# Turning a graph hop's product back: fp32 matmuls with a combining matrix, or transposes with the halves added on VectorE

## The reference, cut to what matters

```python
h0 = x @ W + b
h = h0
for _ in range(10):
    msg = (h * norm_src)[src]
    agg = segment_sum(msg, dst, num_segments=3125)
    h = 0.9 * (agg * norm_dst) + 0.1 * h0
```

## Time and profile before

| what | us |
|---|---|
| median of three runs | 3213.01 |
| lowest and highest run | 3197.84, 3217.87 |
| span of the profiled execution (first to last instruction) | 3198.0 |
| TensorE busy over the span | 2723.7 (85%) |
| VectorE busy | 2250.6 (70%) |
| ScalarE busy | 1612.0 (50%) |
| GpSimd busy | 1512.6 (47%) |

### The profile page before, as it was taken

The page is one execution under the profiler, slowest core; times in us unless marked ns, Lnnn a source line. Parts: engine busy times, 40 slices in busy tenths (PEclk is TensorE's granted clock), DMA queues, the critical chain, the costliest instruction groups (busy, mean ns, idle before and its releaser), DMA issues. The chain is left out here.

```text
span 3198.0 us, 70441 instructions
## 1 busy us (share of the span) xinstructions
PE 2723.7 (85%) x18621; PEld 1834.2 (57%) x18621; DVE 2250.6 (70%) x6702; ACT 1612.0 (50%) x4685; POOL 1512.6 (47%) x1604
## 2 busy tenths in 40 slices
PE   2777777799998499759888888998986999999998
PEld 1566665355554244337777777776874555555556
DVE  6999998566665312657777777777887777777772
ACT  1788887033332000035555555555664666666666
POOL 2121122044443000067777777777405777777770
PEclk6999999899999799869999999999997999999995
DMA  1122222056557755543333333333203555445540
GB/s 38 73 91 89 91 89 89 21 195 204 196 197 257 270 238 238 223 102 80 84 81 81 82 85 79 83 83 82 63 21 98 127 131 131 127 128 130 131 112 12
DMA packets 446966, 378.15 MB, mean 118 GB/s; under 512 B 174376, under 2 KB 385416, under 8 KB 446632
## 3 DMA queue, kind: packets, MB, share of 16 engines
q1 hardware_dynamic: 396184, 315.64, 32.3%
q0 software_dynamic: 40896, 43.60, 6.7%
q10 hardware_dynamic: 9552, 14.75, 1.3%
HBM read 286.75 MB, written 87.03 MB: 117 GB/s over the span
## 5 line engine op out<-in xcount | busy, mean ns | idle before, releaser
L1594 POOL DMA_INDIRECT big<-row_table,src x710 | 675.0, 951 | 217.1 <-issue 171.6
L2080 POOL DMA_INDIRECT big<-message_table,src x542 | 532.6, 983 | 228.2 <-issue 154.2
L2119 PE MATMUL banks<-big 128*128 128x512 f16 x1650 | 422.6, 380 | 8.9 <-DVE big L2194 8.9
L2212 DVE TENSOR_SCALAR big<-big 128x2048 f16<-128x2048 f16 (+2 forms) x396 | 422.4, 1067 | 1.3 <-DMA big<-shifted_keys 0.7
L507 PE MATMUL banks<-work 128*128 128x226 f16 x1197 | 312.3, 261 | 104.2 <-ACT banks L538 41.4
L899 PE MATMUL banks<-big,work 128*128 128x512 f16 (+1 forms) x1750 | 350.0, 359 | 17.0 <-DVE work L1041 17.0
L964 POOL TENSOR_TENSOR work<-work 128x400 f16<-128x400 f32 x196 | 180.2, 945 | 280.5 <-DVE work L1033 220.3
L1739 DVE TENSOR_REDUCE big<-banks 128x1 f32<-128x256 f32 x451 | 190.2, 422 | 173.1 <-PE banks L1637 159.7
L1637 PE MATMUL banks<-big 97*128 x902 | 303.4, 419 | 0.7
L508 PE MATMUL banks<-work 128*128 128x200 f16 x1197 | 300.5, 251 | 0.0
L509 PE MATMUL banks<-work 128*128 128x200 f16 x1197 | 298.6, 249 | 0.0
(11 more groups left out here) (373 smaller groups left out, 6143.4 us busy)
## 6 DMA issues: line engine op xcount, KB each, us to landing
big<-weights_halves SPq DMA_DIRECT2D x10, 6400.0 KB, 24.0
big<-shifted_keys SPq DMA_DIRECT2D x66, 640.0 KB
weights_dense<-work SPq DMA_DIRECT2D x196, 200.0 KB, 1.9
work<-weights_dense SPq DMA_DIRECT2D x196, 200.0 KB, 2.7
weights_halves<-work SPq DMA_DIRECT2D x98, 400.0 KB, 2.9
big<-q_table SPq DMA_DIRECT2D x451, 64.0 KB
big<-in_ef SPq DMA_DIRECT2D x403, 64.0 KB
big<-in_ea SPq DMA_DIRECT2D x403, 32.0 KB
```

The costliest lines, as they stand in the source:

```text
L1594: po.indirect_dma_start(rows[:, t % RT, s, 0:D], None, x_t.rearrange("a p c -> (a p) c"), bass.IndirectOffsetOnAxis(ap=m.src2[:, s, t:t + ...
L2080: po.indirect_dma_start(G[n % R][:, s, :], None, g_t.rearrange("a p c -> (a p) c"), bass.IndirectOffsetOnAxis(ap=m.src2[:, s, t:t + 1], ax ...
L2119: pe.matmul(psH[q % 2], table[:, a, :, :].rearrange("p s d -> p (s d)"), hot[:, 2 * TE * a:2 * TE * (a + 1)], start=(a == 0), stop=(a == N ...
L2212: dve.tensor_scalar(hot[:, 2 * TE * a:2 * TE * (a + n)], key[q % 2][:, 0:n, :], place[:, BATCHES.index((a, n)):BATCHES.index((a, n)) + 1], ...
```

## The change

The turn-back is done by transposes of 128x128 with the identity (four in a chunk of 512), so that the high halves of 128 nodes stand in 64 columns of the bank and the low halves in the next 64: a bank is now filled with 512 columns and not with 256. ScalarE multiplies in its copy by a per-partition factor `weigh`, 1 in partitions 0 to 63 and 1 / LO in the others. VectorE adds the two halves from PSUM by a tensor_reduce over a strided view (innermost the two halves, 64 columns apart) ahead of the mix. `comb` is no longer made.

```diff
+        self.weigh = self.colsN[:, 7, 10:11]
...
-            dve.tensor_copy(comb[0:D, :], m.ident[0:D, 0:D])
-            chain(dve.tensor_scalar(comb[D:P, :], m.ident[D:P, D:P], 1.0 / LO, None, ALU.mult))
+            dve.memset(m.weigh[0:D, :], 1.0)
+            dve.memset(m.weigh[D:P, :], 1.0 / LO)
...
-                    ins = pe.matmul(m.PB[6 + c % 2][0:k, i * D:(i + 1) * D], rt[c % 2][:, i * P:i * P + k], comb,
-                                    start=True, stop=True)
+                    ins = pe.transpose(m.PB[6 + c % 2][0:k, i * P:(i + 1) * P], rt[c % 2][:, i * P:i * P + k], m.ident[:, :])
...
-                    nc.scalar.copy(rt[c % 2][:, 0:width(c)], m.PB[c % 4][:, 0:width(c)]).then_inc(copied, 1)
+                    nc.scalar.activation(rt[c % 2][:, 0:width(c)], m.PB[c % 4][:, 0:width(c)], ACT.Copy, scale=m.weigh).then_inc(copied, 1)
...
-                    ps = m.PB[6 + c % 2][0:rows, 0:g * D].rearrange("p (a d) -> p a d", a=g)
+                    ps = m.PB[6 + c % 2][0:rows, 0:g * P].rearrange("p (a s d) -> p a d s", a=g, s=2)
                     tc = tmp[0:rows, 0:g, :]
...
+                    chain(dve.tensor_reduce(tc, ps, op=ALU.add, axis=X))
                     if last:
-                        chain(dve.tensor_tensor(tc, ps, sp_(c1n), ALU.mult))
+                        chain(dve.tensor_tensor(tc, tc, sp_(c1n), ALU.mult))
...
-                        chain(dve.tensor_tensor(tc, ps, sp_(c1s), ALU.mult))
+                        chain(dve.tensor_tensor(tc, tc, sp_(c1s), ALU.mult))
...
-            per = 4 * NDC
+            per = 5 * NDC
```

More of the change, by code:

```diff
@@ L682, in stage_layer0_start @@
         ones16 = small(2).bitcast(F16)
-        comb = small(3)
         buf = [m.work2[0:D, i * DC:(i + 1) * DC] for i in range(2)]
@@ L842, in stage_layer0_hops @@
         z = [m.zbuf(0), m.zbuf(1)]
-        comb = m.small(3)
         h0, hs0 = m.node(1), m.node(2)
```

## The result

| | before | with the change |
|---|---|---|
| median, us (13 runs each) | 3213.01 | 3225.41 |
| lowest and highest run | 3197.31, 3226.26 | 3210.22, 3251.76 |
| span of the profiled execution | 3198.0 | 3222.9 |
| the ten hops in it | 434.90 | 448.24 |

What follows compares the result with a forecast made beforehand. The prediction took TensorE and a nearly equally long loop through the other engines as the bound. Loop growth of 17.6 us plus 17 us of clock falls, +35 in all on the median 3213.01, gave 3248 us, range 3220 to 3280.

Steps and rivals of the forecast that it cites:

- The bound: In the ten hops: TensorE and the loop nearly equally long, so lengthening the loop is paid.
- the loop: In a hop: turn-back, mix, low halves, store, load, landing, high halves, copy, later turn-back; +0.50 us per turn-back and mix.
- TensorE's term: Turn-back on TensorE: four transposes, 0.44 us, for fp32 matmuls, 0.83 us; -0.40 us per full chunk.
- The copy's term: ScalarE's copy from PSUM, made an activation with per-partition scale: +0.085 us per copy.
- The reduce's term: VectorE's added tensor_reduce per chunk ahead of the mix: 0.86 us, +0.90 with the gap (ends 0.73 and 1.10).
- The walk over the hops: Loop growth: odd hops +1.57 us, even +0.59, degree matmul of four even hops +1.37; together +17.6 us.
- The clock's term: Longer TensorE gaps lower the granted clock: one new fall in each of seven hops, 2.4 us each, +17 us.
- The signs: Trace marks of being right, such as odd hops of 42.5 us or more and granted clock under 0.97.
- rival B: In the hops the loop grows but the clock holds: 3213 + 18 = 3231 us; chance 0.21.
- Rival A: TensorE's saving of 25 us in the hops arrives in full: 3188 us; chance 0.07.
- C: Rival: reduce of 1.06 us or more and two clock falls in each hop: +65 us, 3278 us; chance 0.15.
- D: Rival: transposes not shorter on TensorE, each loop passage losing 0.40 us more: 3253 us; chance 0.07.

Runs made afterwards that it cites:

- e6: The kernel before with ScalarE taking the high halves of chunk c behind the copy of c + 1: 3196.6 us, ratio 0.9944.
- e8: The kernel before with copies ahead of high halves, bank 4 for the small turn-back and the degree matmul a chunk later: 3189.0 us, ratio 0.9919.
- e3: The kernel before with only ScalarE's copy made a scaled activation and 1/LO taken out of the combining matrix: 3219.8 us, ratio 1.0027.
- e2: The kernel before with a useless tensor_reduce of 512 SBUF elements ahead of each mix (128 in the last chunk): 3251.9 us, ratio 1.0128.
- e5: The changed kernel with ScalarE taking the high halves of chunk c behind the copy of c + 1: 3221.9 us, ratio 1.0030.
- e4: The changed kernel with the small turn-back in its own bank 4 and the degree matmul one product later: 3213.6 us, ratio 0.9993.
- e10: e5 with seven needless matmuls ahead of turn-back 4 and eight ahead of the small one, except in the last hop: 3217.5 us, ratio 1.0011.
- e1: The changed kernel without the tensor_reduce, low halves left out of the result: 3198.4 us, ratio 0.9955.
- e7: The changed kernel with copies ahead of high halves, bank 4 for the small turn-back and the degree matmul a chunk later: 3195.6 us, ratio 0.9964.
- e9: e7 without GpSimd's wait for the mix ahead of its low halves: 3254.0 us, ratio 1.0126.

## Why the prediction was right, and where it failed

**The bound.** Right. TensorE's busy time fell by 26 us and the kernel got slower, and e6 shows the loop by undoing one link of it. "TensorE and this loop are nearly equally long now" holds too: it took e8, with ScalarE's order turned and the hop's end freed, to bring TensorE to 97%.

**TensorE's term** (-0.40 per chunk). Right: 0.44 us for 0.83.

**The copy's term** (0.085). Measured 0.10 (682 ns for 581), in the change and in e3.

**The reduce's term** (0.86, step 0.90). Mis-sized: 0.691, so a step of 0.73, my low end. I had the rows of a strided SBUF read and put PSUM half way to them; a contiguous SBUF read (e2) and the strided PSUM read cost the same to 5 ns. My walk over the loop gives +12.3 with that number and 0.10 for the copy, and the stage grew by 13.3. (The middle of my two rates, 0.69 and 1.06, is 0.87 and not 0.86; that changes nothing.) The note on cachelines that I weighed, of the Trainium skill (SBUF — State Buffer, section on the DMA port swizzle), I had read as putting the reduce at my upper end. Of PSUM the note speaks for matmuls only, and the measurement decides against my reading for this pattern.

**The walk over the hops.** The sum came out, its parts did not, so the nearness of 12.3 and 13.3 is in part luck. In two hops the clock held in both kernels, and +1.96 was forecast for either: hop 4 grew by 2.77 (41.29 to 44.06) and hop 8 by 1.40 (42.28 to 43.68). Odd hops were forecast at +1.57: hop 5 grew by 2.99 and hop 3 by 2.03, each with a fall near its end or its start, and hop 7 by nothing (42.04, behind a fall, to 41.86). Hop 6 got shorter (44.33 to 43.41); before, it had a wait of 2.33 us and a fall. The slack that I gave turn-back 4 of even hops came from one hop. The trace of before showed such a wait in three other even hops (1.46 in hop 0, 0.32 in hop 2, 2.33 in hop 6), and my walk passed over them. This is its row in hop 4 with the change; the second row is that hop's end and the third the degree matmul in hop 6, both forecast at 1.8:

```profile
836.86 0.66 PE L882 MATMUL banks<-ident,work 128*128 128x128 f32 x4 [1.00 <-ACT work L933]
...
840.42 0.27 PE L882 MATMUL banks<-ident,work 128*64 128x128 f32 x1 [1.59 <-DVE work L1032]
...
891.67 0.38 PE L890 MATMUL banks<-work 128*128 128x1 f32 x2 [1.59 <-DVE work L992]
```

**The clock's term** (seven new falls at 2.4 us, +17). This is the step that failed, and it holds most of the error. Of the 23 us by which I was off, 17 are this term and 5 the reduce's. The gaps did grow: 1.8 us at the hop's end and at the degree matmul were expected, and both mostly measured 1.59 to 1.72. At turn-back 4 of an odd hop 2 us were expected, and 0.82, 1.31, 3.29, 0.94 and none were measured. At turn-back 2, where I had forecast none, they were 1.14 to 2.38 in hops 0 to 8, where eight of the nine had been under 0.5. The clock did not follow. The stage has four falls behind its start (near 662, 750, 880 and 1040 us) where it had three (660, 914 and 1030): one more, not seven more. Twenty gaps of TensorE behind 630 us are longer than the 1.46 of the earlier trace rows, and four of them had a fall. A gap longer than the 1.46 of the earlier trace rows in TensorE's timeline (and the one of 3.29, which a fall did follow), and the windows at the first:

```profile
823.47 0.66 PE L882 MATMUL banks<-ident,work 128*128 128x128 f32 x4 [2.38 <-ACT work L933]
823.96 5.56 PE L897 MATMUL banks<-big,work 128*128 128x512 f16 x25
...
880.39 1.11 PE L882 MATMUL banks<-ident,work 128*128 128x128 f32 x4 [3.29 <-ACT work L933]
```

```profile
820.00:824.00 4.00, 1.62 (x11) 0.82 (x9) 1.56 (x2) 1.65 (x4) 2.12 (x3) 1.00 0.84 289
824.00:828.00 4.00, 4.00 (x21) 1.82 (x19) 3.67 (x8) 0.98 (x2) 1.22 (x3) 1.00 0.64 204
```

2.38 us idle and full clock behind it. I had taken one pair of rows, a fall behind 1.46 and none behind 0.98, for a threshold in the length of a single gap. Most of those that a fall followed were longer or had company: 3.29 here; 2.34 at 660.86 and 0.68 at 664.43; 2.06 at 749.28 and 0.95 at 752.85; 2.22 and 2.00 in e5. Length alone does not sort them: in e4 2.73 at 813.81 had no fall, and 1.98 at 978.86 had one. The price was too high as well, by e10: about 1 us where I took 2.4.

**The signs.** Met: the transposes at 0.44, the idle time before turn-backs and the degree matmul at 41.5 + 12.3 + 6.4 = 60 us, and the granted clock at 0.96. Not met: the one odd hop with full clock (hop 7) took 41.86 and not 42.5 or more, and VectorE's wait for turn-backs, which I expected hardly to change, fell from 111.0 to 78.2 us: the longer chain took its time out of that wait.

**The rivals.** What came is rival B, at 0.21, with the reduce at its low end: 3213 + 12 = 3225. Rival A is what e1 shows a part of; its condition, a landing that follows the product, is met in none of the chains that I read. C and D fell with the reduce's 0.69 and the transposes' 0.44.

## What to carry to other kernels

Before a saving on the busiest engine is counted, look at what its short waits stand behind: here an engine with 94% of the stage gave away 26 us and got none of it back. A copy was queued behind a transfer that hung on another engine's work, and the same change made that work longer. Work moved from the busiest engine to one at 62% lay on the path and cost more there (0.73 us) than it saved (0.39), and turning the order of one engine (e6, 14 us) was worth more than the edit itself. A transpose beat the fp32 matmul for the same 128 nodes on TensorE (0.11 us for 0.21), but a matmul with a combining matrix also does the adding, and that has to be in the sum.

## What was not expected of the hardware

- A tensor_reduce from PSUM whose every read jumps 64 columns took 691 ns for 512 elements, as one over 512 neighbours in SBUF did (686). The column sums in SBUF, with their strided view of 400 elements, took 826.
- Gaps of TensorE of 1.8 to 2.4 us that stood alone were not followed by a lower granted clock four times in the change, nor was one of 2.47 in e7; but one of 2.08 in e5, at 791 us, was, and so were those of 2.59 and 2.74 in e7. In e4 one of 2.73 was not. Two close together in e5 were all six times. What decides it was not isolated.
- GpSimd's tensor_tensor beside VectorE's doubled it (425 to 911 ns in e9). In small it is there in e7 and e8 too, at the first instruction of the mix that reads two operands from SBUF: the multiply in e7 (468 ns), and in e8, whose multiply reads PSUM (423), the add behind it (477). In the change both take 425.

Open: why even and odd hops grew so unevenly, which turns on when single tiles landed, was not followed further. Two versions with transposes in which TensorE's saving could still arrive were not tried: one whose column sums are taken off VectorE, and one in which the copy of chunk 5 also stands ahead of the tiles.
